# Adaptive-norm transformer block: residual transposes, last value product and last probability copies in another order

## The reference

```python
ada = (timestep_embed @ ada_w + ada_b)[:, None, :]
shift1, scale1, gate1, shift2, scale2, gate2 = jnp.split(ada, 6, axis=-1)
x1 = _ln(x) * (1.0 + scale1) + shift1
qkv = (x1 @ qkv_w + qkv_b).reshape(Bc, Tc, 3, H, DH)      # 16 heads of 128
attn = jnp.einsum('bthd,bshd->bhts', q, k) * scale
attn = jax.nn.softmax(attn, axis=-1)
attn_out = jnp.einsum('bhts,bshd->bthd', attn, v).reshape(Bc, Tc, INNER)
attn_out = attn_out @ out_w + out_b
x = x + gate1 * attn_out
x2 = _ln(x) * (1.0 + scale2) + shift2
h = jax.nn.gelu(x2 @ ffn_w1 + ffn_b1, approximate=False)   # 1024 wide
x = x + gate2 * (h @ ffn_w2 + ffn_b2)
...
h = jnp.square(jax.nn.relu(x @ ternary(W_fc).T))           # second block
return x_in + rms_norm(h) @ ternary(W_proj).T
```

## Time and profile before

| | |
|---|---|
| median of 3 runs | 366.54 us (366.31 to 367.02) |
| profiled execution | 366.18 us, span 364.4 us |
| PE busy | 347.1 us, 95% of the span |
| DVE busy | 218.1 us, 60% |
| ACT busy | 197.6 us, 54% |
| POOL busy | 109.9 us, 30% |
| granted PE clock | 0.996 of full speed on average |

### The profile page before, as it was taken

One profiled execution on the slowest core, in us unless ns is written; L12 is line 12 of the kernel. 1 busy time (PEld: TensorE's weight loads), 2 busy tenths in 40 slices (PEclk: granted clock), 3 DMA queues, 4 the chain that ended last, 5 costly groups with the idle time before them and its releaser, 6 DMA issues.

```text
span 364.4 us, 5719 instructions
## 1 busy us (share of the span) xinstructions
PE 347.1 (95%) x1968; PEld 299.6 (82%) x1968; DVE 218.1 (60%) x401; ACT 197.6 (54%) x516; POOL 109.9 (30%) x98
## 2 busy tenths in 40 slices
PE   2989999999999999999999999999989999999994
PEld 2779888888888888888888888888867788789873
DVE  5772337436444743643664354377988876577894
ACT  1554654544555454545555445655485745776681
POOL 2532224321742232272313245327336200000101
PEclk9999999999999999999999999999999999999998
DMA  7923031000303100030300003010000000000011
GB/s 244 374 80 116 1 117 58 2 0 2 116 0 115 58 0 0 0 115 4 111 0 0 0 0 116 2 58 3 0 0 2 1 2 0 0 2 1 2 58 58
DMA packets 11778, 16.52 MB, mean 45 GB/s; under 512 B 673, under 2 KB 7921, under 8 KB 11761
## 3 DMA queue, kind: packets, MB, share of 16 engines
q1 hardware_dynamic: 11760, 16.30, 13.4%
HBM read 15.25 MB, written 1.05 MB: 45 GB/s over the span
## 4 chain that ended last, share of the span: by engine, by line
PE 86%; DVE 7%; ACT 3%; issue 2%; DMA 1%; SPq 0%; POOL 0%; DVEq 0%; ACTq 0%
PE bank L939 19%; PE bank L941 19%; PE bank L940 19%; PE bank L966 8%; PE bank L985 7%; PE bank L974 4%; PE bank L1202 3%; PE bank L1212 2%; PE bank L1053 2%; PE bank L1062 1%; DMA hbuf<-in_L_cond_ada_w_dram 1%; DVE hid_lo L674 1%; DVE prob L645 1%; DVE hbuf L875 1%; ACT xfull L437 1%
## 5 line engine op out<-in xcount | busy, mean ns | idle before, releaser
L339 POOL TENSOR_TENSOR prob<-prob,rinv 128x512 f32<-128x512 f32 x32 | 33.3, 1041 | 149.8 <-DVE rinv L753 149.8
L477 ACT ACTIVATE prob<-bank,nbias 128x128 f32<-128x128 f32 x128 | 45.2, 365 | 39.1 <-DVE nbias L747 39.1
L744 DVE TENSOR_REDUCE negmax<-bank 128x4 f32<-128x512 f32 x32 | 22.1, 690 | 73.6 <-PE bank L966 73.6
L939 PE MATMUL bank<-x_hi,wqk_hi 128*128 128x512 f32 x128 | 53.5, 418 | 0.0
L941 PE MATMUL bank<-x_hi,wqk_lo 128*128 128x512 f32 x128 | 50.3, 393 | 0.0
L940 PE MATMUL bank<-x_lo,wqk_hi 128*128 128x512 f32 x128 | 49.9, 390 | 0.0
L448 ACT ACTIVATE o_hi<-bank,bias 128x512 fp32r<-128x512 f32 x32 | 22.0, 687 | 39.6 <-PE bank L985 39.6
L452 ACT ACTIVATE vals<-bank 128x512 f32<-128x512 f32 x32 | 19.1, 597 | 36.4 <-PE bank L941 36.4
L985 PEld LDWEIGHTS bank<-probT,vals 128*128 128x128 f32 x256 | 33.3, 191 | 3.4 <-DVE probT L678 0.6
L682 DVE TENSOR_SCALAR kT<-bank,bias 128x512 f32<-128x512 f32 x32 | 23.9, 748 | 19.0 <-PE bank L941 19.0
L985 PE MATMUL bank<-probT,vals 128*128 128x128 f32 x256 | 33.9, 275 | 0.2 <-DVE probT L678 0.2
(11 more groups left out here) (147 smaller groups left out, 766.6 us busy)
## 6 DMA issues: line engine op xcount, KB each, us to landing
raw_qk<-in_L_cond_qkv_w_dram SPq DMA_DIRECT2D x8, 512.0 KB, 4.8
raw_v<-in_L_cond_qkv_w_dram SPq DMA_DIRECT2D x4, 512.0 KB, 3.9
raw_o<-in_L_cond_out_w_dram SPq DMA_DIRECT2D x4, 512.0 KB, 3.5
xt<-in_x_dram SPq DMA_DIRECT2D x2, 512.0 KB, 4.7
xr<-in_L_cond_ada_w_dram SPq DMA_DIRECT2D x1, 1024.0 KB, 9.3
raw_w<-in_L_cond_ffn_w_dram SPq DMA_DIRECT2D x2, 512.0 KB, 7.3
t_raw<-in_L_ffn_W_fc_dram SPq DMA_DIRECT2D x4, 256.0 KB, 3.6
t_raw<-in_L_ffn_W_proj_dram SPq DMA_DIRECT2D x4, 256.0 KB, 3.8
```

What stands on the lines that cost most here:

```text
L339: nc.gpsimd.tensor_tensor(e, e, rinv[:, j % 2, :].unsqueeze(2).broadcast_to([P, SQ, P]), ALU.mult).then_inc(norm_done, 1)
L477: e = nc.scalar.activation(prob[:, j % 2, s, :], bank[BS][:, s * P:(s + 1) * P], ACT.Exp, bias=nbias[:, j % 2, s:s + 1], scale=SCALE, accu ...
L744: nc.vector.tensor_reduce(negmax[:, j % 2, :], bank[BS][:, :].rearrange("p (s t) -> p s t", s=SQ), axis=AX.X, op=ALU.max, negate=True).the ...
L939: nc.tensor.matmul(dst, ah, bh, start=start and n == 0, stop=False)
```

## The change

Only units 30 and 31 and the first feed-forward half are touched.

- PE, unit 30: the transposes of quad 0's yT stand between the query and key products instead of behind both. Their halves go to banks 5 and 4 instead of 4 and 5.
- PE, unit 31: the transposes of the residual leave their place ahead of the output product. The order is now output product of unit 29, value product of unit 30, transposes of the normalised x (no longer waiting for the copy of the residual), transposes of the residual into banks 5 and 3 (waiting for the exponentials of unit 31), transposes of the last probabilities.
- PE, feed-forward: the value product of unit 31 stands behind chunk 0 instead of ahead of it; the second yT transposes also wait for the residual copy.
- VectorE, units 30 and 31: o_lo comes ahead of negmax. The probability copies are gone. In unit 30 the residual is added ahead of the reciprocal, in unit 31 x is normalised ahead of the reciprocal.
- ScalarE: copies the probabilities of units 29 and 30 ahead of the exponentials of units 30 and 31, and those of unit 31 behind the modulation. The load of the GELU table moves behind that. The residual copy moves behind GELU 1.
- GpSimd: the third low part of w2 moves from unit 30 to unit 31.

The tail of the diff, cut to what the steps speak of:

```diff
@@ gpsimd, last group
-                    if j in W2_AT:
-                        w2_lo_part(W2_AT[j])
+                    for n in {2: (0,), 3: (1,), 7: (2, 3)}.get(j, ()):
+                        w2_lo_part(n)
@@ scalar
+            def keep_p(i):
+                act.wait_ge(t_mm, i + 1)
+                nc.scalar.activation(probT[:, :, :].rearrange("p s t -> p (s t)"), bank[BV][:, :], ACT.Copy).then_inc(p_done, 1)
+
             def unit(G, j, vs, more, last=False):
                 i = UG * G + j
+                if last and j >= UG - 2:
+                    keep_p(i - 1)
                 act.wait_ge(nb_done, i + 1)
...
-                if last and j == UG - 1:
-                    copy_xrT(0, bank[0:2])
-
-                    act.wait_ge(half_set, 1)
-                    nc.scalar.activation(scratch[:, :], neg_half[:, :], ACT.Gelu)
...
             modulate(2, SHIFT2, SCALE2, bank[0:2])
+            keep_p(NU - 1)
+
+            act.wait_ge(half_set, 1)
+            nc.scalar.activation(scratch[:, :], neg_half[:, :], ACT.Gelu)
             o_hi_part(NG - 1, UG - 1)
...
                 ffn1_gelu(0, c)
+                if c == 1:
+                    copy_xrT(0, (bank[BO + 1], bank[BS]))
@@ vector
                 first = isinstance(i, int) and i == 0
+                end = last and j >= UG - 2
+                if end:
+                    o_lo_part(*before(G, j, 2))
                 dve.wait_ge(s_mm, i + 1)
...
-                if not first:
+                if not first and not end:
                     keep_p(i - 1)
+                if last and j == UG - 2:
+                    add_residual(0)
+                if last and j == UG - 1:
+                    normalise(2, xr)
                 dve.wait_ge(exp_done, i + 1)
...
-            modulate(2, SHIFT2, SCALE2, bank[0:2], lambda: keep_p(NU - 1))
+            modulate(2, SHIFT2, SCALE2, bank[0:2])
@@ tensor
                 project(bank[BQ], 0, a, quad).then_inc(q_mm, 1)
+                if between:
+                    between()
                 project(bank[BK], 1, a, quad).then_inc(k_mm, 1)
...
                 if known and i == NU - 1:
-                    transpose_xr(0, bank[0:2])
                     out_product(*before(G, j, 2))
                     pv(*before(G, j, 1))
-                    pe.wait_ge(p_done, i)
+                    transpose_x(2, bank[0:2])
+                    pe.wait_ge(exp_done, NU)
+                    transpose_xr(0, (bank[BO + 1], bank[BS]))
                     transpose_p(i, j % 2)
-                    pe.wait_ge(xrT_done, 1)
-                    transpose_x(2, bank[0:2])
                     return
...
             out_product(NG - 1, UG - 2)
-            pv(NG - 1, UG - 1)
...
                 ffn1(0, c)
+                if c == 0:
+                    pv(NG - 1, UG - 1)
                 if c == 1:
                     out_product(NG - 1, UG - 1)
                 if c == 4:
+                    pe.wait_ge(xrT_done, 1)
                     transpose_y(1)
```

More of the change, by code:

```diff
@@ L735, in add_residual @@
                     s = slice(quad * SQ + 2 * n, quad * SQ + 2 * n + 2)
-                    m = nc.vector.tensor_tensor(xr[:, s, :].rearrange("p s d -> p (s d)"), bank[BO + n][:, :],
+                    m = nc.vector.tensor_tensor(xr[:, s, :].rearrange("p s d -> p (s d)"), bank[BO + 1 - n][:, :],
                                                 xt[:, s, :].rearrange("p s d -> p (s d)"), ALU.add)
@@ L747, in unit @@
                 nc.vector.tensor_scalar(nbias[:, j % 2, :], negmax[:, j % 2, :], SCALE, None, ALU.mult).then_inc(nb_done, 1)
-                if not isinstance(i, int) or i >= 2:
+                if (not isinstance(i, int) or i >= 2) and not end:
                     o_lo_part(*before(G, j, 2))
-                if not first:
+                if not first and not end:
                     keep_p(i - 1)
+                if last and j == UG - 2:
+                    add_residual(0)
+                if last and j == UG - 1:
+                    normalise(2, xr)
                 dve.wait_ge(exp_done, i + 1)
@@ L756, in unit @@
                     keep_k(G1, j1)
-                    if last and j == UG - 2:
-                        add_residual(0)
                 if j == 5:
@@ L765, in unit @@
                     stats_of(2, xr)
-                if last and j == UG - 1:
-                    normalise(2, xr)
                 if j == 3:
@@ L946, in project, with qk_products @@
                                              x_hi[:, k, cols(quad)], x_lo[:, k, cols(quad)]) for k in range(KD)])
-            def qk_products(G, j):
+            def qk_products(G, j, between=None):
                 a, quad = j % HG, j // HG
@@ L1013, in unit @@
                         pe.wait_ge(v_done, blocks)
-                    qk_products(*((G, j + 1) if j < UG - 1 else (G + 1, 0)))
-                if extra:
-                    extra()
+                    qk_products(*((G, j + 1) if j < UG - 1 else (G + 1, 0)), between=extra)
                 if known and i == NU - 1:
-                    transpose_xr(0, bank[0:2])
                     out_product(*before(G, j, 2))
                     pv(*before(G, j, 1))
-                    pe.wait_ge(p_done, i)
+                    transpose_x(2, bank[0:2])
+                    pe.wait_ge(exp_done, NU)
+                    transpose_xr(0, (bank[BO + 1], bank[BS]))
                     transpose_p(i, j % 2)
-                    pe.wait_ge(xrT_done, 1)
-                    transpose_x(2, bank[0:2])
                     return
@@ L1102, in transpose_y @@
                     for c in range(KD):
-                        m = nc.tensor.transpose(bank[BO + s // 2][:, (s % 2) * D + c * P:(s % 2) * D + (c + 1) * P],
+                        m = nc.tensor.transpose(bank[BO + 1 - s // 2][:, (s % 2) * D + c * P:(s % 2) * D + (c + 1) * P],
                                                 yT[:, c, cols(quad, s)], ident[:, :])
```

## The result

| | before | changed |
|---|---|---|
| median of 11 executions each | 366.58 us (366.31 to 367.12) | 368.63 us (367.35 to 369.87) |
| ratio, with 95% interval | | 1.0051 (1.004 to 1.0061) |
| profiled execution, span | 366.18, 364.4 us | 369.40, 367.6 us |

The changed kernel is slower by 2.05 us, where 0.76 was forecast, and its executions are spread over 2.5 us where those of before lie within 0.8. Two of the eleven took 367.35 and 367.57 us, at a mean granted clock of 0.998; the other nine took 367.96 to 369.87 at 0.990 to 0.995. The forecast describes the two. The mean clock alone does not tell the two kinds apart, as it also takes in what the clock does behind the last matmul: executions of the kernel before have means from 0.993 (366.55 us) to 0.999 (366.90 us).

A forecast was written before the change was run, and what follows sets the result against it. PE, busy 95%, was taken as the bound, so the start of chunk 5 decides the end. The terms 0 + (0.87 - 0.11) + 0 = +0.76 us on 366.54 gave 367.3 us, range 365.9 to 368.0.

The forecast's parts named there:

- Part 1: Up to the value product of unit 29: work only permuted, no gain; that product at 261.53 us.
- Part 2: Unit 31 up to chunk 0: chunk 0 starts 2.1 us earlier, at 271.3; normalising takes 1.38 us.
- Part 3: Last value product, now behind chunk 0: starts 0.87 us later, at 272.77; o_lo(31) ends 0.76 us later.
- Part 4: From o_lo(31) to gated yT: length unchanged at 7.65 us, VectorE and POOL locked to each other.
- Rival A: Faster: both gating multiplications slip in ahead of t_w, yT gated at 280.9, time 365.1 us; chance 14%.
- rival B: No change: PV(31) delayed less, by chunk 0 before 271.0 or VectorE winning t_dn; 366.2 to 366.8 us; chance 18%.
- PE between: PE from unit 31's output product through chunk 4: done at 281.0, then idle 2.0 us, where about 0.6 before.
- The sum: Whole kernel: 0 + (0.87 - 0.11) + 0 = +0.76 us on the median 366.54, giving 367.3.
- C, much slower: the clock: Clock falls to 1.2 GHz around 283, twelve matmuls of chunks 5 and 6 cost 2.7 us more: 370.0; chance 6%.

The follow-up runs named there:

- The experiment on the normalising: Changed kernel with the normalising of x back behind the reciprocal in unit 31, as before the change: 372.22 us, ratio 1.0141.
- The part alone: Kernel before with only the value product of unit 31 moved behind chunk 0: 369.66 us, ratio 1.01.
- both repairs: Changed kernel with unit 31's value product ahead of chunk 0, its copy on VectorE, t_dn ahead of o_lo(31), last w2 high part ahead of o_hi(31): 363.43 us.

## Why the prediction was wrong, step by step

- **Part 1, no gain up to the value product of unit 29**: right, 261.52 against 261.53 forecast.
- **Part 2, chunk 0 2.1 us earlier**: right, 271.28 against 271.3. The normalising took 1.38 us as forecast, PE's idle was 0.96 (1.0). The experiment on the normalising shows what its place carries: 3.5 us, with the w2 low part where the change has it. I had not priced that the w2 low part moved behind the multiplication; as the normalising went ahead of both, it made no difference.
- **Part 3, the last value product 0.87 us and o_lo(31) 0.76 us later**: right, 272.78 and 275.40 (forecast 272.77 and 275.39). The part alone costs 3.0 us, and without it (and with the copy back on VectorE) the change gains 1.8.
- **Part 4, 7.65 us from o_lo(31) to the gating**: right, 283.96 - 276.31 = 7.65. Rival A, that the gating slips in ahead of t_w, is out, and with chunk 0 at 271.28 and t_dn held for 2.26 us so is rival B; t_dn ahead of o_lo(31) shows that GpSimd's hold is real: the gating takes 1.29 us where t_w is done and 3.51 where it is not. That t_up is 0.4 us longer beside a hid_lo, which the prediction puts down to the earlier trace rows, those rows do not show by themselves; the other three t_up of the kernel before took 2.13 us.
- **PE between, 2.0 us of idle**: right, 1.96. GELU 2 ended at 279.25 and not near 279.9, so the residual copies held nothing.
- **The sum**: the executions without a fall average 367.34 against 367.3 predicted. The schedule was right; the step that failed is the clock, which the sum "0 + (0.87 - 0.11) + 0" puts at nothing and rival "C, much slower: the clock" prices at 2.7 us and gives 6%. The runs show executions slower than the schedule in nine to twelve of sixteen, and in the one that can be compared row by row the fall costs 1.52 us. C's 2.7 was too much: it took all twelve matmuls of chunks 5 and 6 at the lower level, but only the first seven ran there, and they started 0.43 us apart where 0.23 is usual. With the long stall filled no execution is as slow, with only the short one filled three of seven are. With the measured fall put in afterwards the same working gives 367.3 + 1.5 = 368.8, against 368.63 measured. What stays open is why the clock fell in some executions of one program and not in others.
- I weighed the clock by two rows, the 2 us of idle around 6 us, where it held, and the end, where it fell within 2 us of the last matmul. The first outweighed the second in my mind, though the second is the one that follows upon dense work. The Trainium skill's page TensorE: Matmul & The Clock Gate (part 1), which has the clock halved by idleness, spoke against the change; the trace agrees (PEclk 0.50 from 286 to 288). It gave the direction, but neither a chance nor a cost for one stall of 2 us.

## What to carry to other kernels

When an instruction is moved into the shadow of another, look at the last thing that hangs on it, not at the gap that it leaves: here 2.1 us won ahead of chunk 0 were lost to an output whose low part stands ahead of 7.65 us of work in which VectorE and GpSimd hold each other up. And a schedule change that leaves PE one wait of 2 us where it had waits of 0.5 us and less can cost more by the clock than by the later schedule (1.5 against 0.76 us here): look at single executions, since times that fall into two groups give it away, compare a profile of each group row by row, and fill the stall with idle transposes to test it, on a chip on which the unfilled kernel runs too.

## What the runs showed of the hardware that was not expected

- The granted clock fell to its 1.2 GHz level behind a single PE wait of 1.96 us in a stretch that was otherwise busy, in some executions and not in others of one and the same program (by their times nine to twelve of sixteen, and three of seven with the shorter wait filled; in rows one fall and one execution without). With PE waits of at most 0.5 us in that stretch, as before had them, and of 1.1 us, in the kernel with only the value product moved back (6 executions), no second group of times appeared. Shorter waits are not safe everywhere: with both repairs the clock fell at 356 us, with PE at work, behind waits of 0.39, 0.59 and 0.19 us and eight matmuls of 2 columns.
- A GpSimd elementwise operation held one VectorE instruction that reads SBUF until it was through, also one with a single tensor input: normalising took 3.18 us instead of 1.38 beside two GpSimd operations of 1.04 and 1.31, its first two instructions about 1.3 us each and the other two 0.40. It goes the other way too: t_up took 2.54 us where VectorE's hid_lo had begun 0.16 us before it, and 2.13 to 2.15 where none had. VectorE's o_lo and the first sum into yT, which read a PSUM bank, took 0.75 and 1.40 us beside GpSimd work as without it.
